# Cross-attention and RWKV layers on one core: GpSimd instead of VectorE computes the third bf16 piece of queries and keys

## The chip, the cores and the metric

The kernel runs on one core of a Trainium2 chip. The metric is the device time of one execution in microseconds (us); less is better. TensorE (PE) multiplies matrices and transposes, VectorE (DVE), ScalarE (ACT) and GpSimd (POOL) do the elementwise work, and SyncE (SP) issues nearly all DMAs. Each engine runs its own list of instructions strictly in order, and semaphores tie the lists together. A blocked instruction blocks everything behind it on its engine.

## The reference, cut to what matters

For each of 8 batches, layer 0 normalises x and the context (layer norm over 128 channels), makes queries, keys and values, does 16-head attention with softmax over 256 positions, and then a feed-forward block. Layer 1 is an RWKV layer: a learned token shift, receptance, key, value, gate and decay, a linear scan in time with an 8x8 state per head, group norm, gate, and a feed-forward block.

```
q = layer_norm(x + pos);  kv = layer_norm(ctx + pos)
Q, K, V = q @ Wq, kv @ Wk, kv @ Wv
ctx = softmax(Q @ K.T / sqrt(8)) @ V
r = ctx @ Wo + q;  x1 = gelu(layer_norm(r) @ W1 + b1) @ W2 + b2 + r
...
state = k*v + w*state;  out_t = r_t @ (u*k*v + state)     # 32 heads of 8, one step a token
```

The scores Q @ K.T are computed from bf16 pieces: Q and K (f32) are each split into three bf16 numbers, high, middle and low, and six products of such pieces are stacked along the contraction.

## The kernel before

The work of a batch is cut into five stages: a (normalise, queries, keys, values and their split), g (the maximum score of each row, the guard that keeps the exponential in range), h (scores, exponential, weighted sums, feed-forward), r (token shift, projections, scan) and o (read-out, group norm, feed-forward, store). The batches are pipelined: while batch n is in stage a or g, batch n-1 is in h and r, batch n-2 in o.

The order of work is written out by hand. `BEGIN` holds the tick at which each batch's stage begins, and `AT` the offset of each operation in its stage. Every engine's program walks through all ticks and emits what is due. A tick is no time: it decides only which instruction comes before which one on the same engine.

The split in stage a goes over four instructions, on 128x512 elements, queries and keys side by side. ACT `high` (L620) copies the product out of the PSUM bank `a_even` to `parts[:, 0]`. DVE `left` (L826) is the rest, `a_even - high`. ACT `middle` (L634) rounds it to `parts[:, 1]`. The last one, which this case is about, is the tensor_tensor of L829: `parts[:, 2] = left - parts[:, 1]`, f32 minus bf16 to bf16. SP's `spill` (L337) then copies the three pieces into `q_stack` and `k_stack` by 12 DMAs a batch, piece 2 last; it waits for the semaphore `s_parts` there.

On POOL stand, before the change: `zsum` (L774), the input plus positions, which is the first operation of stage a and which PE's `centre` (L397) waits for; `rstd_a`, `rstd_h`, `rstd_r`, `rstd_o` and `hrs` (powers of -0.5 on few elements); `kv` (L790, L791), and `rst_low` (L795).

PE's part that matters here is in this order in the first three batches: centre of batch 0, the rest of its stage a, centre and rest of stage a of batch 1, the 16 score pairs of stage g of batch 0 (L424, with DVE's row maxima `top`, L834, between them), the guard of batch 0, centre of batch 2. Before centre of batch 1 PE waits for three things:

```
pe.wait_ge(s_zsum, a.n + 1)
if a.n == 1:
    pe.wait_ge(s_left, 1)
    pe.wait_ge(s_v_padded, 1)
```

In stage r, DVE's `sx` (L882, the difference of neighbouring tokens, two inputs in SBUF), `xx` (L885) and PE's `maa1` (L509) follow one another; in stage o DVE's `yo` (L988) makes the output from two inputs in SBUF.

Of the kernel before, what the change touches and what calls it, by code (L numbers as in the profile page):

```python
# [9 lines left out]
ALU = mybir.AluOpType  # L10
# [36 lines left out]
for _n, _w in WEIGHTS:  # L47
# [17 lines left out]
        "SP": {"load": 0, "spill": (2322, 2430, 2430)},  # L65
        "PE": {"centre": 1792, "turn_nrm": 1951, "qk": 2014, "v": 2032},
        "ACT": {"dev": 1861, "nrm": 1920, "affine": 1985, "high": 2040, "v_pad": 2062, "middle": 2162},
        "POOL": {"zsum": 1726, "rstd_a": 1996},
        "DVE": {"var_a": 1808, "left": 2072, "parts": 2352},
    },  # L70
    "g": {
        "SP": {"guard": 380},
# [56 lines left out]
def due(at, engine, op, i=None):  # L129

    return PLACES.get((engine, op, i, at))


def ticks():

    times = [place[3] for place in PLACES]
    return range(min(times), max(times) + 1)


def build(nc, x, ctx_in, weights, vecs, pos, first, out):  # L140
    with ExitStack() as stack:
        def sb(name, shape, dt=F32):
            return stack.enter_context(nc.sbuf_tensor(name, shape, dt))
# [32 lines left out]
        def s0(batch):  # L176

            return initial[:, batch.n, 4:4 + 2 * S1].rearrange("p (h d) -> p h d", h=2)
# [3 lines left out]
        zsum = sb("zsum", [128, 2, T])  # L182
        devsq = sb("devsq", [128, 4, 128])
        squares = sb("squares", [128, 4])
        var_a = sb("var_a", [128, 4])
        rstd_a = sb("rstd_a", [128, 4])
# [3 lines left out]
        parts = sb("parts", [128, 3, 2, T], BF16)  # L190
        left = sb("left", [128, 2, T])
# [113 lines left out]
        def dma(batch, count=1):  # L305

            return batch.k * (16 * count) + 16 * count
# [446 lines left out]
        @block.gpsimd  # L754
        def _(pool):
            pool.memset(mhalf[:, :], -0.5).then_inc(s_setup, 1)
            pool.memset(th[:, :, :], 0.0).then_inc(s_setup, 1)
            for n in range(3):
                pool.memset(k_stack[n][:, :, :], 1.0).then_inc(s_setup, 1)
            for p in range(2):  # L760

                pool.memset(dec_rep[p][:, :, :, 0], 0.0).then_inc(s_zero, 1)

                pool.memset(yo[p][:, 0:1], 0.0).then_inc(s_stored[p], 16)
            pool.memset(x2[:, 0:1], 0.0).then_inc(s_done, 1)
            pool.wait_ge(s_const, CONSTS)
            pool.wait_ge(s_setup, SETUP)

            for at in ticks():
                if a := due(at, "POOL", "zsum"):  # L770
                    pool.wait_ge(s_x_in[a.p], dma(a, 2))
                    if a.n >= 1:
                        pool.wait_ge(s_centred, a.n)
                    pool.tensor_tensor(zsum[:, :, :], xin[a.p][:, :, :], pe_tab[:, None, :].broadcast_to([128, 2, T]), ALU.add).then_inc(s_zsum, 1)  # L774
                if a := due(at, "POOL", "rstd_a"):
                    pool.wait_ge(s_vareps, a.n + 1)
                    pool.tensor_tensor(rstd_a[:, :], var_a[:, :], mhalf[:, 0:4], ALU.pow).then_inc(s_rstd, 1)  # L777
                if h := due(at, "POOL", "rstd_h"):
                    pool.wait_ge(s_hvareps, h.n + 1)
                    pool.tensor_tensor(rstd_h[:, :], var_h[:, :], mhalf[:, 0:2], ALU.pow).then_inc(s_hrstd, 1)  # L780
                if r := due(at, "POOL", "rstd1"):
                    pool.wait_ge(s_var1, r.n + 1)
                    pool.tensor_tensor(rstd_r[:, :], var_r[:, :], mhalf[:, 0:1], ALU.pow).then_inc(s_rstd1, 1)
                for half in range(2):
                    if r := due(at, "POOL", "kv", half):
                        pool.wait_ge((s_v_rep_low, s_v_rep_high)[half], (r.n + 1) * 16)
                        pool.wait_ge(s_rk_sb, r.n + 1)
                        if r.n == 0:
                            pool.wait_ge(s_initial, 16)
                        pool.tensor_copy(kv[:, half, :, 0], s0(r)[:, half, :]).then_inc(s_kv, 1)  # L790
                        pool.tensor_tensor(kv[:, half, :, 1:NT], v_rep[:, half, :, 1:NT], rk[r.p][:, 1, half, None, 0:NT - 1].broadcast_to([128, S1, NT - 1]),  # L791
                                           ALU.mult).then_inc(s_kv, 1)
                if r := due(at, "POOL", "rst_low"):
                    pool.wait_ge(s_st, r.n * 2 + 1)
                    pool.tensor_tensor(st[:, 0, :, :], st[:, 0, :, :], rk[r.p][:, 0, 0, None, :].broadcast_to([128, S1, NT]), ALU.mult).then_inc(s_rst_low, 1)  # L795
                if o := due(at, "POOL", "hrs"):
                    pool.wait_ge(s_hvareps1, o.n + 1)
                    pool.tensor_tensor(hrs[:, :], hvar[:, :], mhalf[:, :], ALU.pow).then_inc(s_hrs, 1)  # L798
                if o := due(at, "POOL", "rstd2"):
                    pool.wait_ge(s_var2, o.n + 1)  # L800
                    pool.tensor_tensor(rstd_o[:, :], var_o[:, :], mhalf[:, 0:1], ALU.pow).then_inc(s_rstd2, 1)  # L801
# [3 lines left out]
        def _(dve):  # L805
# [14 lines left out]
            for at in ticks():  # L820
# [3 lines left out]
                if a := due(at, "DVE", "left"):  # L824
                    dve.wait_ge(s_high, a.n + 1)
                    dve.tensor_tensor(flat(left[:, :, :]), a_even[:, :], parts[:, 0].rearrange("p s t -> p (s t)"), ALU.subtract).then_inc(s_left, 1)  # L826
                if a := due(at, "DVE", "parts"):
                    dve.wait_ge(s_middle, a.n + 1)
                    dve.tensor_tensor(parts[:, 2], left[:, :, :], parts[:, 1], ALU.subtract).then_inc(s_parts, 1)  # L829

                for head in range(H0):
                    if g := due(at, "DVE", "top", head):
# [250 lines left out]
```

## Time and profile before

| what | value |
|---|---|
| device time, median of 3 runs | 441.82 us (441.0 to 442.71) |
| device time of the profiled execution | 440.58 us |
| its span in the profile | 438.4 us |
| TensorE | busy 72% of the span |
| VectorE | busy 65% of the span |
| ScalarE | busy 52% of the span |
| GpSimd | busy 36% of the span |
| mean granted clock of TensorE | 0.886 |

The span runs from the first to the last profiled instruction; the device time of the same execution is 2.2 us longer. In rows of the timeline a number xN behind an instruction means N of them merged, and the brackets at the end tell how long the engine had been idle and what ended the idle time.

### The profile page before, as it was taken

The page shows a single profiled execution, that of the slowest core. Times are in us where ns is not written, and L with a number is a line of the kernel's source. Part 1 is how long each engine was busy: PE and PEld are TensorE (multiplying, and loading weights), DVE is VectorE, ACT ScalarE, POOL GpSimd, SP SyncE. Part 2 cuts the span into 40 slices and gives each one's busy share as a digit, 9 for nine tenths or more (in the row PEclk, how much of TensorE's full clock was granted, in tenths as well). Part 3 has the DMA queues.
Part 4 walks back from the last instruction along what each step waited for, and adds up shares of the span by engine and source line. Part 5 has one row for each costly group of instructions (what it writes and reads, how often), then busy time and mean ns, then how long its engine had stood idle before and what let it go on. Part 6 is the DMA issues. An engine that isn't in the chain of part 4 may idle for free.

```text
span 438.4 us, 6463 instructions
## 1 busy us (share of the span) xinstructions
PE 317.3 (72%) x2320; PEld 203.3 (46%) x2320; DVE 285.3 (65%) x610; ACT 229.3 (52%) x585; POOL 158.4 (36%) x102
## 2 busy tenths in 40 slices
PE   1447587688598979896988798879878866664135
PEld 1321333455354655565555555555655554552013
DVE  5119057177569868985798698869877546747331
ACT  0540364763795488548845975665477564033010
POOL 6220200100754083428144614544072454417310
PEclk9965569699989999998999999989999998688555
DMA  8433020002600430061007000700400140041000
GB/s 243 203 98 88 27 55 20 1 25 62 122 24 1 113 70 1 1 143 40 2 1 168 27 0 21 176 0 2 110 13 2 22 99 0 0 106 40 0 0 12
DMA packets 23695, 23.44 MB, mean 53 GB/s; under 512 B 3568, under 2 KB 21360, under 8 KB 23536
## 3 DMA queue, kind: packets, MB, share of 16 engines
q1 hardware_dynamic: 23520, 19.57, 18.8%
q10 hardware_dynamic: 144, 3.47, 2.0%
q8 instruction: 18, 0.29, 0.3%
q14 instruction: 13, 0.11, 0.1%
HBM read 14.51 MB, written 2.10 MB: 38 GB/s over the span
## 4 chain that ended last, share of the span: by engine, by line
PE 43%; DVE 20%; ACT 17%; issue 15%; POOL 5%; POOLq 0%; ACTq 0%; DVEq 0%
PE o_bank L378 4%; PE h_sum L457 4%; DVE mixed L896 4%; DVE top L834 4%; PE r_one L371 4%; PE r_two L371 3%; PE h_even L490 3%; ACT L669 2%; ACT dec_rep L722 2%; PE r_one L384 2%; PE r_two L509 2%; DVE mixed L905 2%; ACT probs L643 2%; PE a_odd L424 2%; PE h_odd L445 2%
## 5 line engine op out<-in xcount | busy, mean ns | idle before, releaser
L798 POOL TENSOR_TENSOR hrs<-hvar,mhalf 128x32 f32<-128x32 f32 x8 | 43.5, 5439 | 52.3 <-DVE hvar L950 52.3
L834 DVE TENSOR_REDUCE top<-a_even 128x2 f32<-128x512 f32 x64 | 44.0, 687 | 11.4 <-PE a_even L424 6.3
L643 ACT ACTIVATE probs<-h_odd 128x512 f32<-128x512 f32 x64 | 38.3, 598 | 23.0 <-PE h_even L445 17.9
L834 DVE TENSOR_REDUCE top<-a_odd 128x2 f32<-128x512 f32 x64 | 43.9, 685 | 6.1 <-PE a_odd L424 5.8
L643 ACT ACTIVATE probs<-h_even 128x512 f32<-128x512 f32 x64 | 38.1, 595 | 14.3 <-PE h_odd L445 7.4
L927 DVE TENSOR_TENSOR_SCAN st<-dec_rep,v_rep 128x1024 f32<-128x1024 f32 x16 | 38.0, 2409 | 3.0 <-POOL v_rep L791 3.0
L791 POOL TENSOR_TENSOR v_rep<-v_rep,rk 128x1016 f32<-128x1016 f32 x16 | 37.6, 2348 | 0.0
L457 PE MATMUL h_sum<-probs,v_pad 128*32 128x256 f32 x512 | 35.1, 393 | 0.0
L795 POOL TENSOR_TENSOR st<-st,rk 128x1024 f32<-128x1024 f32 x8 | 30.2, 3770 | 7.6 <-DVE st L927 7.6
L424 PE MATMUL a_even<-k_stack,q_stack 62*128 62x256 bf16 x128 | 26.4, 289 | 6.0 <-DVE top L834 3.3
L424 PE MATMUL a_odd<-k_stack,q_stack 62*128 62x256 bf16 x128 | 26.5, 290 | 5.4 <-DVE top L834 5.4
L777 POOL TENSOR_TENSOR rstd_a<-var_a,mhalf 128x4 f32<-128x4 f32 x8 | 13.3, 1659 | 40.0 <-DVE var_a L823 40.0
L445 PE MATMUL h_odd<-q_stack,k_stack 64*128 64x256 bf16 x128 | 25.7, 282 | 1.3 <-ACT probs L643 0.9
L445 PE MATMUL h_even<-q_stack,k_stack 64*128 64x256 bf16 x128 | 25.7, 282 | 0.6 <-ACT probs L643 0.3
L801 POOL TENSOR_TENSOR rstd_o<-var_o,mhalf 128x1 f32<-128x1 f32 x8 | 4.4, 550 | 53.8 <-DVE var_o L967 53.8
L790 POOL COPY v_rep<-initial 128x8 f32<-128x8 f32 x16 | 4.6, 290 | 52.3 <-DMA v_rep<-values 27.6
L384 PE MATMUL r_one<-th,W 128*128 128x128 f32 x96 | 15.8, 304 | 6.8 <-ACT th L689 6.0
L826 DVE TENSOR_TENSOR left<-a_even,parts 128x512 f32<-128x512 f32 x8 | 5.5, 689 | 22.5 <-ACT parts L620 22.3
L397 PE MATMUL a_even<-W,zsum 128*128 128x128 f32 x64 | 10.9, 322 | 12.7 <-POOL zsum L774 8.0
L457 PEld LDWEIGHTS h_sum<-probs,v_pad 128*32 128x32 f32 x512 | 13.5, 110 | 13.0 <-issue 7.2
L384 PEld LDWEIGHTS r_one<-th,W 128*128 128x128 f32 x96 | 12.8, 203 | 10.8 <-ACT th L689 8.4
L780 POOL TENSOR_TENSOR rstd_h<-var_h,mhalf 128x2 f32<-128x2 f32 x8 | 5.8, 731 | 31.7 <-DVE var_h L857 31.6
(157 smaller groups left out, 778.0 us busy)
## 6 DMA issues: line engine op xcount, KB each, us to landing
v_rep<-values SPq DMA_DIRECT2D x16, 511.5 KB, 5.4
W<-in_weights ACTq DMA_DIRECT2D x1, 3392.0 KB, 11.5
q_stack<-parts SPq DMA_DIRECT2D x48, 64.0 KB, 3.4
k_stack<-parts SPq DMA_DIRECT2D x48, 64.0 KB, 2.7
xin<-in_x SPq DMA_DIRECT2D x8, 128.0 KB, 2.3
xin<-in_ctx SPq DMA_DIRECT2D x8, 128.0 KB, 2.7
values<-vt SPq DMA_DIRECT2D x8, 128.0 KB, 1.8
out<-yo SPq DMA_DIRECT2D x8, 128.0 KB, 3.9
```

Source lines behind the costliest of these rows:

```text
L371: mm = pe.matmul(dst[:, m * 128:(m + 1) * 128], w(name, half * E + m * 128, 128), src[:, half, :], start=half == 0, stop=half == 1)
L378: mm = pe.matmul(dst, src[:, half, :], w(name, half * E, E), start=half == 0, stop=half == 1)
L384: mm = pe.matmul(dst[:, half * 128:(half + 1) * 128], w(f"maa_w2_{group}", half * 128, 128), th[:, group // 4, :], start=True, stop=True)
L424: mm = pe.matmul(a_score[head % 2][:, j * T:(j + 1) * T], q_stack[g.ring][e:e + TOP_ROWS, head // 2, j * 128:(j + 1) * 128], k_stack[g.rin ...
L445: mm = pe.matmul(h_score[head % 2][:, j * T:(j + 1) * T], k_stack[h.ring][e:e + GUARD_ROWS, head // 2, j * 128:(j + 1) * 128], q_stack[h.r ...
L457: mm = pe.matmul(h_sum[quad * QUAD:(quad + 1) * QUAD, half * T:(half + 1) * T], v_pad[h.ring][:, j, HEAD_ORDER[four * 4 + quad], :], probs ...
L643: act.activation(flat(probs[turn % PROBS][:, :, :]), h_score[HEAD_ORDER[turn] % 2][:, :], ACT.Exp, scale=SCORE_SCALE).then_inc(s_probs, 1)
L791: pool.tensor_tensor(kv[:, half, :, 1:NT], v_rep[:, half, :, 1:NT], rk[r.p][:, 1, half, None, 0:NT - 1].broadcast_to([128, S1, NT - 1]), A ...
L795: pool.tensor_tensor(st[:, 0, :, :], st[:, 0, :, :], rk[r.p][:, 0, 0, None, :].broadcast_to([128, S1, NT]), ALU.mult).then_inc(s_rst_low, 1)
L798: pool.tensor_tensor(hrs[:, :], hvar[:, :], mhalf[:, :], ALU.pow).then_inc(s_hrs, 1)
L834: dve.tensor_reduce(top[:, :, H0 // 2 * (head % 2) + head // 2], a_score[head % 2][:, :].rearrange("p (a t) -> p a t", a=2), AX.X, ALU.max ...
L927: dve.tensor_tensor_scan(flat(st[:, half, :, :]), flat(dec_rep[r.p][:, half, :, :]), flat(kv[:, half, :, :]), 0.0, ALU.mult, ALU.add).then ...
```

## The change

The subtraction that makes the low piece leaves DVE's list and goes to POOL's, with the same operands, the same wait for `s_middle` and the same update of `s_parts`. Its offset in stage a changes from 2352 to 2478.

```
-        "POOL": {"zsum": 1726, "rstd_a": 1996},
-        "DVE": {"var_a": 1808, "left": 2072, "parts": 2352},
+        "POOL": {"zsum": 1726, "rstd_a": 1996, "parts": 2478},
+        "DVE": {"var_a": 1808, "left": 2072},
...
+                if a := due(at, "POOL", "parts"):
+                    pool.wait_ge(s_middle, a.n + 1)
+                    pool.tensor_tensor(parts[:, 2], left[:, :, :], parts[:, 1], ALU.subtract).then_inc(s_parts, 1)
...
-                if a := due(at, "DVE", "parts"):
-                    dve.wait_ge(s_middle, a.n + 1)
-                    dve.tensor_tensor(parts[:, 2], left[:, :, :], parts[:, 1], ALU.subtract).then_inc(s_parts, 1)
```

What this does to the lists: PE, ACT and SP keep theirs row for row, DVE's loses 8 rows and POOL's gains 8. POOL's list near the start, from the first zsum on, before the change (zsum of batch 0, rstd_a of batch 0, zsum of batch 1, and so on):

```order
15 L774 TENSOR_TENSOR zsum<-xin,pe_tab 128x512
16 L777 TENSOR_TENSOR rstd_a<-var_a,mhalf 128x4
17 L774 TENSOR_TENSOR zsum<-xin,pe_tab 128x512
18 L777 TENSOR_TENSOR rstd_a<-var_a,mhalf 128x4
19 L774 TENSOR_TENSOR zsum<-xin,pe_tab 128x512
```

The same place in the list of the changed kernel, where L780 is the moved subtraction:

```order
15 L774 TENSOR_TENSOR zsum<-xin,pe_tab 128x512
16 L777 TENSOR_TENSOR rstd_a<-var_a,mhalf 128x4
17 L780 TENSOR_TENSOR parts<-left,parts 128x512
18 L774 TENSOR_TENSOR zsum<-xin,pe_tab 128x512
19 L777 TENSOR_TENSOR rstd_a<-var_a,mhalf 128x4
20 L780 TENSOR_TENSOR parts<-left,parts 128x512
21 L774 TENSOR_TENSOR zsum<-xin,pe_tab 128x512
```

So parts of batch 0 now stands ahead of zsum of batch 1, and parts of batch 1 ahead of zsum of batch 2. From batch 2 on it stands behind the next batch's zsum, here for batch 4 (ahead of hrs of batch 0):

```order
37 L786 TENSOR_TENSOR rstd_r<-var_r,mhalf 128x1
38 L774 TENSOR_TENSOR zsum<-xin,pe_tab 128x512
39 L780 TENSOR_TENSOR parts<-left,parts 128x512
40 L801 TENSOR_TENSOR hrs<-hvar,mhalf 128x32
41 L804 TENSOR_TENSOR rstd_o<-var_o,mhalf 128x1
```

On DVE, the place from which parts of batch 3 is taken, before the change (the `top` rows are the row maxima of stage g of batch 2, `mixed` and `gate` are of stage r of batch 0):

```order
73 L834 TENSOR_REDUCE top<-a_odd 128x2
74 L905 TENSOR_TENSOR mixed<-mixed,xt 128x5x128 x2
75 L829 TENSOR_TENSOR parts<-left,parts 128x512
76 L834 TENSOR_REDUCE top<-a_even 128x2
77 L834 TENSOR_REDUCE top<-a_odd 128x2
78 L834 TENSOR_REDUCE top<-a_even 128x2
```

Without it, the maxima follow `mixed` directly; nothing else moves on DVE.

## Rows read from the trace of the kernel before

**Rows 1.** The page: busy time and share by engine; the last chain by engine.

```profile
PE 317.3 (72%) x2320; PEld 203.3 (46%) x2320; DVE 285.3 (65%) x610; ACT 229.3 (52%) x585; POOL 158.4 (36%) x102
...
PE 43%; DVE 20%; ACT 17%; issue 15%; POOL 5%; POOLq 0%; ACTq 0%; DVEq 0%
```

**Rows 2.** Timeline, 5 to 60 us: start us, length us, engine, line, operation.

```profile
6.57 1.26 POOL L774 TENSOR_TENSOR zsum<-xin,pe_tab 128x512 f32<-128x512 f32 x1
7.97 2.04 PE L397 MATMUL a_even<-W,zsum 128*128 128x128 f32 x8 [7.97 <-POOL zsum L774]
...
13.91 1.26 POOL L774 TENSOR_TENSOR zsum<-xin,pe_tab 128x512 f32<-128x512 f32 x1
...
20.86 0.63 ACT L634 ACTIVATE parts<-left 128x512 bf16<-128x512 f32 x1
...
21.08 1.13 PE L397 MATMUL a_even<-W,zsum 128*128 128x128 f32 x8 [0.75 <-ACT v_pad L628]
21.52 0.69 DVE L829 TENSOR_TENSOR parts<-left,parts 128x512 bf16<-128x512 f32 x1 [0.70 <-ACT parts L634]
...
45.13 2.05 PE L397 MATMUL a_even<-W,zsum 128*128 128x128 f32 x8 [1.04 <-DVE guard L842]
```

**Rows 3.** Same timeline, DVE in the maxima of batch 0.

```profile
36.77 0.69 DVE L834 TENSOR_REDUCE top<-a_odd 128x2 f32<-128x512 f32 x1
37.38 0.68 DVE L829 TENSOR_TENSOR parts<-left,parts 128x512 bf16<-128x512 f32 x1
...
37.98 0.69 DVE L834 TENSOR_REDUCE top<-a_even 128x2 f32<-128x512 f32 x1
```

**Rows 4.** Busy us (and instructions) by window; PEclk is TensorE's granted clock.

```profile
core 0: us, PE busy (x) PEld busy (x) DVE busy (x) ACT busy (x) POOL busy (x), PEclk, DMA share, GB/s
21.00:24.20 3.20, 1.13 (x8) 0.97 (x8) 0.86 (x2) 1.64 (x9) 0.53 (x1) 1.00 0.34 87
24.40:31.00 6.60, 3.98 (x12) 2.99 (x12) 0.12 (x1) 2.76 (x7) 1.52 (x2) 0.50 0.41 110
```

**Rows 5.** Timeline of DVE around parts of batch 3 and of batch 7.

```profile
101.36 0.69 DVE L829 TENSOR_TENSOR parts<-left,parts 128x512 bf16<-128x512 f32 x1
...
104.18 0.69 DVE L834 TENSOR_REDUCE top<-a_even 128x2 f32<-128x512 f32 x1 [0.94 <-PE a_even L424]
...
268.94 0.68 DVE L829 TENSOR_TENSOR parts<-left,parts 128x512 bf16<-128x512 f32 x1
...
270.47 0.69 DVE L834 TENSOR_REDUCE top<-a_even 128x2 f32<-128x512 f32 x1 [0.51 <-PE a_odd L424]
```

**Rows 6.** Timeline of ACT (middle of batch 6) and of POOL (hrs behind it).

```profile
216.79 0.65 ACT L634 ACTIVATE parts<-left 128x512 bf16<-128x512 f32 x1
...
219.97 5.44 POOL L798 TENSOR_TENSOR hrs<-hvar,mhalf 128x32 f32<-128x32 f32 x1 [6.32 <-DVE hvar L950]
```

**Rows 7.** Timeline of POOL and DVE: yo beside POOL's st, and alone.

```profile
162.90 3.55 POOL L795 TENSOR_TENSOR st<-st,rk 128x1024 f32<-128x1024 f32 x1
...
165.02 1.72 DVE L988 SCALAR_TENSOR_TENSOR yo<-y,x 128x256 f32<-128x256 f32 x1
...
207.92 0.55 DVE L988 SCALAR_TENSOR_TENSOR yo<-y,x 128x256 f32<-128x256 f32 x1
```

**Rows 8.** Timeline, middle, sx and maa1: batches 3 and 0, then 4 and 1.

```profile
89.98 0.63 ACT L634 ACTIVATE parts<-left 128x512 bf16<-128x512 f32 x1
...
91.40 0.42 DVE L882 TENSOR_TENSOR sx<-xt 128x256 f32<-128x256 f32 x1 [0.40 <-ACT xt L683]
...
91.86 0.61 DVE L885 SCALAR_TENSOR_TENSOR xx<-sx,vec,xt 128x128 f32<-128x128 f32 x2
...
92.53 0.60 PE L509 MATMUL r_two<-xx,W 128*128 128x128 f32 x3
...
129.55 0.62 ACT L634 ACTIVATE parts<-left 128x512 bf16<-128x512 f32 x1
...
131.04 0.42 DVE L882 TENSOR_TENSOR sx<-xt 128x256 f32<-128x256 f32 x1
...
132.24 0.38 PE L509 MATMUL r_two<-xx,W 128*128 128x128 f32 x1
```

**Rows 9.** The page, a costly group of POOL: busy us, mean ns.

```profile
L791 POOL TENSOR_TENSOR v_rep<-v_rep,rk 128x1016 f32<-128x1016 f32 x16 | 37.6, 2348 | 0.0
```

## The prediction

> **What bounds the kernel now.** I read the page first. No engine is full: TensorE is busy 72%, VectorE 65%, GpSimd 36% [rows 1]. So a change matters only where a wait ends last, and that has to be read place by place. The chain that ended last runs 43% over PE and 20% over DVE, and only 5% over POOL [rows 1]: on average POOL has room for one more instruction a batch, and DVE is the scarcer engine. An average says nothing of the place, however, so I went to the timeline next, at each of the eight places where parts leaves DVE and each of the eight where POOL takes it up. The places are of two kinds. In the first batches nothing is pipelined yet and everything hangs on one thread; from batch 2 on, four engines work on three batches at once.
>
> **The start, batch 0.** Before the change, zsum of batch 1 ran at 13.91 us, far ahead of its use; PE's centre of batch 1 started at 21.08, released by v_pad of batch 0 [rows 2]. In the changed order POOL has parts of batch 0 between rstd_a of batch 0 and that zsum. Parts waits for ACT's middle, which starts at 20.86 and takes 0.63, so it ends at 21.49 [rows 2]. POOL can start some 0.08 later (an estimate: a semaphore's hop), at 21.57. Queued behind the waiting instruction is zsum of batch 1, and behind that centre of batch 1, and PE's list has nothing else to offer.
>
> How long is parts on POOL? The trace has no such instruction there. The nearest row is zsum, two inputs, 512 elements: 1.26 us [rows 2]. Below it is half of kv, 2.348/2 = 1.17 us for 508 elements [rows 9]; above it half of st, 3.55/2 = 1.78 us [rows 7], which is lengthened by a neighbour. I take 1.26; the bf16 operand is not in any row, and 1.17 and 1.78 stay for the range. The Trainium skill (GPSIMD Engine Reference, section 3.1) gives 1.96 times DVE's duration for an f32 tensor_tensor; with this kernel's 0.69 us on DVE that would be 1.35, an estimate that would add 0.09 to the sum.
>
> So parts ends at 21.57 + 1.26 = 22.83, zsum of batch 1 at 22.83 + 1.26 = 24.09, and PE starts 0.14 later (zsum of batch 0 ended at 6.57 + 1.26 = 7.83, PE started at 7.97 [rows 2]), at 24.23 instead of 21.08: **+3.1 us**. Everything that follows on PE in these batches hangs on this: stage a of batch 1, then the maxima of batch 0, then guard, then centre of batch 2. I found nothing outside this thread that the work waits for here, so what is lost shifts the whole rest.
>
> **The clock at that place.** Centre of batch 1 took 1.13 us, while the same eight matmuls took 2.04 and 2.05 in batches 0 and 2 [rows 2]. The windows say why: granted clock 1.00, which is 2.4 GHz, from 21.0 to 24.2, after PE had been busy with stage a of batch 0, and 0.50, or 1.2 GHz, from 24.4 on, after PE had done only 1.13 us of work in those 3.2 us [rows 4]. The late centre starts at 24.2, after a stretch with no work at all. I expect it at the lower clock: 2.05 - 1.13 = **+0.9 us**. Its bounds are 0 and 0.9, as another execution may have its changes of clock elsewhere. That the cold stretch later on moves along with the work is an assumption that costs nothing either way on average.
>
> **Batch 1.** Here the move pays. In the maxima of batch 0 DVE goes from one top to the next without a gap: 36.77, parts at 37.38, top at 37.98 [rows 3]. Taking parts out brings the next top forward by 37.98 - 37.38 = **-0.6 us**, and the guard, which ends the stage, with it. On POOL, parts of batch 1 and zsum of batch 2 come later by some 13 us, but centre of batch 2 starts only at 45.13 and waits for DVE's guard [rows 2]: cover of 7 us and more, so nothing.
>
> **Batches 3 to 7, DVE.** Is the 0.6 earned again in each? After parts of batch 3 (101.36) DVE does two maxima and then stands idle for 0.94 us until PE delivers (104.18) [rows 5]. So without parts it would only stand idle for 1.5. The five batches look alike: within three rows behind parts DVE waits for PE or ACT, in batch 7 for 0.51 us (parts at 268.94, the waiting top at 270.47) [rows 5]. PE has the long block of projections in front of its next score pair, and that is what DVE waits for. Batch 2 is like that too. The gain there is nothing, with an upper bound of 0.6 each.
>
> **Batches 3 to 7, POOL.** Parts now waits for middle ahead of hrs. The tightest is batch 6: middle ends at 216.79 + 0.65 = 217.44, parts at 217.44 + 0.08 + 1.26 = 218.78, hrs starts at 219.97 [rows 6]. The cover is 1.2 us, and it would take an instruction of 2.4 us to use it up. SP issues piece 2 as early as before or earlier. Nothing.
>
> **A collision on the way.** yo, two inputs in SBUF, took 1.72 us when it started while POOL's st was running, and 0.55 when it was alone; it ended at 166.74, or 0.29 behind st's end at 166.45 [rows 7]. So a DVE instruction of this kind stands still until POOL's has finished. The moved instruction reads and writes SBUF all along, so whom does it meet? In batch 3 middle ends at 90.61, POOL has 90.69 to 91.95, and sx with its two inputs in SBUF starts at 91.40 [rows 8]. It would end at 91.95 + 0.28 = 92.23 instead of 91.82. xx ends at 92.47 and maa1 starts at 92.53 [rows 8], so 0.06 of the 0.41 is slack: +0.35. In batch 4 middle ends at 130.17, POOL has 130.25 to 131.51, sx starts at 131.04 and would end at 131.79 instead of 131.46: 0.33, less about 0.13 of slack ahead of maa1 at 132.24 [rows 8], +0.2. In batches 5 to 7 middle ends after sx has run, and I count nothing. Together **+0.55 us**, with bounds of 0 (sx is not held) and, with 1.78 us on POOL, some 0.5 more in each of the two, 1.6.
>
> The Trainium skill (SBUF — State Buffer, section "Who interferes with whom") says the same as a rule: a VectorE instruction with two SBUF inputs and a GpSimd instruction that reads SBUF share a port, and whoever starts first holds it for the whole instruction. It speaks against this change, and by it the term would be as above; without it the term would be 0 and the sum 3.4.
>
> **The sum.** 3.1 + 0.9 - 0.6 + 0.55 = 3.95, say +4.0 us. The profiled execution took 440.58 us (span 438.4): it would take 444.6 (span 442.4). It lies 1.2 below the median of the runs shown, 441.82; the median becomes **445.8 us**, or 0.9% more. What a measurement of this kernel can tell from no change is about 0.5%, or 2.2 us.
>
> **The rivals.**
> 1. Only the wait at the start counts: the clock's change falls kindly and sx is not held. Then 3.1 - 0.6 = +2.5, so 444.3, and some slack that I took for none may take a part: 443.0 to 444.3, around the border of 0.5%. For it: the clock is seen in one execution, the collision is read from another instruction. Chance 0.17.
> 2. The other side: DVE is the bound after all. If the 0.6 is earned in each of the seven batches 1 to 7 (every row that follows parts moves PE's next block), the move is worth 7 x 0.6 = 4.2, against 3.1 at the start: -1.1, so 440.7, faster though hard to measure. It decides if DVE's gaps behind parts are gaps that PE owes to an earlier maximum. Against it are the gaps of 0.94 and 0.51 us, which end with PE's matmuls that stand behind a block without a gap [rows 5]. Chance 0.05.
> 3. The subtraction is slow on POOL with bf16 operands, 1.78 us or more, and meets more DVE instructions. Then the start costs 3.6, the collisions 1.6: 3.6 + 0.9 - 0.6 + 1.6 = +5.5, so 447.3 and up. For it: no row has bf16 on POOL. Chance 0.08.
>
> My forecast holds the remaining 0.70, from 444.3 to 447.
>
> **How the numbers follow.** The predicted time is that of the forecast, 445.8. The range goes down to 443.3, into rival 1, and up to 447.6, into rival 3; rival 2 and the tails stay out. Slower by over 0.5% (above 444.0): the forecast, rival 3, and a little of rival 1, 0.79. Within 0.5%: most of rival 1, half of rival 2 and what I overlook, 0.17. Faster: 0.04.
>
> **What would show it.** In the changed kernel's profile POOL's parts of batch 0 starts at about 21.6 and lasts 1.2 to 1.8, zsum of batch 1 ends near 24.1, and PE's second centre starts near 24.2, released by POOL, and takes 2.05 (right) or 1.13 (no clock term). Centre of batch 2 starts near 48.5 instead of 45.13; if it starts at 46 or before, the start is wrong. sx of batch 0 and of batch 1 takes about 0.8 instead of 0.42. Behind the place of parts DVE's gaps are longer by 0.6. The distance from centre of batch 2 to the end stays within 1 us of the old one; should it shrink by 3 us, rival 2 is right.

## The result, and the profile after

The changed kernel took 446.56 us (median of 4 runs, 446.06 to 448.43), the kernel before 441.41 in the runs beside it: ratio 1.0102, with a 95% interval of 1.0058 to 1.0146. Run once more with other runs of before beside it, it gave 1.0145 (1.0111 to 1.0179), 447.89 against 442.04 us. It is slower, by 5 to 6 us (5.15 and 5.85).

The page of the changed kernel, busy time by engine, is hardly different from that of before [rows 1]: DVE has 8 instructions and 5 us less, POOL 8 instructions and 9 us more. The averages don't show where the 5.6 us more of span are from.

```profile
span 444.0 us, 6463 instructions
PE 320.5 (72%) x2320; PEld 205.8 (46%) x2320; DVE 280.2 (63%) x602; ACT 229.1 (52%) x585; POOL 167.4 (38%) x110
L780 POOL TENSOR_TENSOR parts<-left,parts 128x512 bf16<-128x512 f32 x8 | 9.2, 1156 | 39.9 <-ACT parts L634 39.9
```

The third line is the moved instruction among the costly groups: 1.16 us on POOL, and POOL sat idle for 39.9 us in all ahead of it, waiting for ACT's middle. Idle time of POOL costs nothing by itself. It costs where something needed is queued behind. The timeline of the start, which answers to [rows 2], shows that place:

```profile
20.87 0.63 ACT L634 ACTIVATE parts<-left 128x512 bf16<-128x512 f32 x1
21.58 1.15 POOL L780 TENSOR_TENSOR parts<-left,parts 128x512 bf16<-128x512 f32 x1 [7.63 <-ACT parts L634]
22.69 1.26 POOL L774 TENSOR_TENSOR zsum<-xin,pe_tab 128x512 f32<-128x512 f32 x1
24.00 2.07 PE L397 MATMUL a_even<-W,zsum 128*128 128x128 f32 x8 [3.67 <-POOL zsum L774]
...
48.99 2.05 PE L397 MATMUL a_even<-W,zsum 128*128 128x128 f32 x8 [1.04 <-DVE guard L842]
```

POOL stands still from 13.95 to 21.58, since parts of batch 0 waits at the head of its queue. zsum of batch 1, which ran at 13.91 before, runs at 22.69, and the releaser of PE's second centre is now POOL's zsum instead of ACT's v_pad: 24.00 instead of 21.08. The third centre starts at 48.99 instead of 45.13. Between these two executions the start is thus 3.9 us longer; how much of that is the change and how much the clock that each of them happened to have is worked out below.

Two more places answer to rows of before. DVE around the place of parts of batch 3 and batch 7, as in [rows 5]:

```profile
107.13 0.69 DVE L834 TENSOR_REDUCE top<-a_even 128x2 f32<-128x512 f32 x1 [1.55 <-PE a_even L424]
...
276.05 0.69 DVE L834 TENSOR_REDUCE top<-a_even 128x2 f32<-128x512 f32 x1 [0.84 <-PE a_odd L424]
```

The gaps were 0.94 and 0.51 and are now 1.55 and 0.84. DVE is done earlier and waits the longer for PE (in batch 7, DVE's next instruction, agg, also waits 0.17 for ACT). And parts, sx and maa1 in batches 3/0 and 4/1, as in [rows 8]:

```profile
93.33 1.16 POOL L780 TENSOR_TENSOR parts<-left,parts 128x512 bf16<-128x512 f32 x1 [1.89 <-ACT parts L634]
94.04 0.73 DVE L882 TENSOR_TENSOR sx<-xt 128x256 f32<-128x256 f32 x1 [0.40 <-ACT xt L683]
...
95.48 1.27 PE L509 MATMUL r_two<-xx,W 128*128 128x128 f32 x8 [0.32 <-DVE xx L885]
...
134.41 1.16 POOL L780 TENSOR_TENSOR parts<-left,parts 128x512 bf16<-128x512 f32 x1 [1.55 <-ACT parts L634]
...
135.21 0.64 DVE L882 TENSOR_TENSOR sx<-xt 128x256 f32<-128x256 f32 x1
```

sx takes 0.73 and 0.64 instead of 0.42. Both times it ends 0.28 us behind POOL's parts (94.77 behind 94.49, 135.85 behind 135.57).

### The profile page after: what moved, and what is told of

It is laid out like the page before. It is cut to its first block, busy times and chain, and to the rows that moved or that the text cites. A ratio compares the mean times of both kernels' runs of the same rounds, so it can differ in the third digit from the quotient of the medians.

```text
span 444.0 us, 6463 instructions
## 1 busy us (share of the span) xinstructions
PE 320.5 (72%) x2320; PEld 205.8 (46%) x2320; DVE 280.2 (63%) x602; ACT 229.1 (52%) x585; POOL 167.4 (38%) x110
## 4 chain that ended last, share of the span: by engine, by line
PE 43%; DVE 19%; ACT 18%; issue 14%; POOL 5%; POOLq 0%; ACTq 0%; DVEq 0%
PE o_bank L378 4%; DVE mixed L896 4%; PE h_sum L457 4%; DVE top L834 4%; PE r_one L371 4%; PE r_two L371 3%; PE h_even L490 3%; ACT L669 2%; ACT dec_rep L722 2%; PE r_one L384 2%; PE r_two L509 2%; DVE mixed L905 2%; ACT probs L643 2%; PE h_odd L445 2%; ACT devsq L603 2%
## 5 line engine op out<-in xcount | busy, mean ns | idle before, releaser
L780 POOL TENSOR_TENSOR parts<-left,parts 128x512 bf16<-128x512 f32 x8 | 9.2, 1156 | 39.9 <-ACT parts L634 39.9
L777 POOL TENSOR_TENSOR rstd_a<-var_a,mhalf 128x4 f32<-128x4 f32 x8 | 13.3, 1659 | 26.3 <-DVE var_a L826 26.3
L397 PE MATMUL a_even<-W,zsum 128*128 128x128 f32 x64 | 11.8, 342 | 15.6 <-POOL zsum L774 11.6
L829 DVE TENSOR_TENSOR left<-a_even,parts 128x512 f32<-128x512 f32 x8 | 5.5, 690 | 22.6 <-ACT parts L620 22.2
L603 ACT ACTIVATE devsq<-a_even 128x128 f32<-128x128 f32 x32 | 8.3, 277 | 19.6 <-PE a_even L397 19.6
```

## The experiments

Theory: the loss is made at one place, zsum of batch 1 waiting behind parts of batch 0. Rivals: POOL's slower instruction and its meetings with DVE cost all along the pipeline; or DVE's relief gives something back there.

**e8_pool_0_first** is the kernel before with parts of batch 0 alone moved, to the same place as in the change. **e2_wait_only** moves nothing and only makes POOL wait at that place.

```
# e8_pool_0_first, against the changed kernel
-                if a := due(at, "POOL", "parts"):
+                if (a := due(at, "POOL", "parts")) and a.n in (0,):
...
+                if (a := due(at, "DVE", "parts")) and a.n not in (0,):
# e2_wait_only, against the kernel before, ahead of zsum
+                    if a.n in (1, 2):
+                        pool.wait_ge(s_parts if a.n == 1 else s_middle, a.n)
```

> The kernel before with parts of batch 0 alone on POOL, ahead of zsum of batch 1 as in the change; all other parts on DVE at their old places. If the start makes the whole loss: second centre at 24.0, +2.9 us and +0.9 of clock, so +3.9 us, 445 to 446, ratio 1.008 to 1.011, about what the whole change costs. Rival: less than half of it, under 443.5.

> The kernel before, parts on DVE, with two waits more on POOL: zsum of batch 1 waits for parts of batch 0 on DVE, zsum of batch 2 for middle of batch 1. Nothing is moved. Start theory: parts of batch 0 ends on DVE at 22.2, zsum of batch 1 at 23.6, the second centre starts at 23.7 instead of 21.1, at the lower clock: +2.6 and +0.9, so +3.5 us, 444.5 to 445.5, ratio 1.007 to 1.010. Rival (the loss comes from the instruction on POOL): no change, 441 to 442.

e8 gave a ratio of 1.0096 (1.0058 to 1.0134), 446.18 us: one instruction of eight, moved, costs as much as the first measurement of the whole change (1.0102), though less than the second (1.0145). e2 gave 1.0070 (1.0042 to 1.0097), 444.51 us, with no work moved at all. Its timeline (in this kernel's line numbers parts on DVE is L831, zsum L776):

```profile
21.53 0.69 DVE L831 TENSOR_TENSOR parts<-left,parts 128x512 bf16<-128x512 f32 x1 [0.70 <-ACT parts L634]
22.39 1.26 POOL L776 TENSOR_TENSOR zsum<-xin,pe_tab 128x512 f32<-128x512 f32 x1 [8.45 <-DVE parts L831]
23.70 2.08 PE L397 MATMUL a_even<-W,zsum 128*128 128x128 f32 x8 [3.38 <-POOL zsum L776]
```

It is 0.3 us less late than the change, as DVE's parts is 0.47 shorter than POOL's and the hop to POOL a little longer. So of the 2.92 us by which the changed kernel's second centre is late, 2.62 come with the wait in POOL's queue alone, and 0.30 with the instruction being on POOL.

**e1_order** undoes nothing but the order: on POOL, parts of batches 0 and 1 goes behind the next zsum.

```
                     for batch in BATCHES:
-                        yield (engine, op, i, BEGIN[stage][batch.n] + offset), batch
+                        late = 200 if (op == "parts" and batch.n < 2) else 0
+                        yield (engine, op, i, BEGIN[stage][batch.n] + offset + late), batch
```

> The changed kernel with one thing undone: on POOL, parts of batches 0 and 1 stands behind zsum of the next batch instead of ahead of it (batches 2 to 7 as in the change). Start theory: the loss comes from zsum of batch 1 waiting behind parts of batch 0. Then the second centre is back near 21.1 us at the high clock, centre of batch 2 near 44.7 (0.2 to 0.6 earlier than before, since DVE's maxima have no parts between them), and the time is 0 to 1 us over before, by the collisions alone: 441 to 442.5, ratio 0.998 to 1.003. Rival (POOL's slower instruction and its collisions with DVE make the loss all along): it stays near the changed kernel, 444 to 446.5, ratio over 1.006.

1.0021 (0.9986 to 1.0055), 442.95 us: no difference that can be told, with all eight parts on POOL. In its profile (centre is L398 here) centre is back, released by v_pad:

```profile
13.93 1.26 POOL L775 TENSOR_TENSOR zsum<-xin,pe_tab 128x512 f32<-128x512 f32 x1
...
21.10 1.13 PE L398 MATMUL a_even<-W,zsum 128*128 128x128 f32 x8 [0.75 <-ACT v_pad L629]
```

One part of the expectation failed: its third centre starts at 45.15 and not near 44.7, no earlier than in the first trace of before (45.13). The section on the clock says why.

**e3_pool_2to7** and **e5_left_out** look at the pipelined part: parts on POOL in batches 2 to 7 alone (as e8, with that set and DVE for the rest); and parts of batches 2 to 7 on no engine.

```
# e5_left_out, against the kernel before
-                if a := due(at, "DVE", "parts"):
+                if (a := due(at, "DVE", "parts")) and a.n < 2:
...
-                        sp.wait_ge((s_high, s_middle, s_parts)[part], a.n + 1)
+                        sp.wait_ge((s_high, s_middle, s_parts if a.n < 2 else s_middle)[part], a.n + 1)
```

> Parts of batches 0 and 1 stays on DVE, that of batches 2 to 7 is on POOL as in the change. Start theory: the start is as before, the collisions with sx in batches 3 and 4 cost 0.3 and 0.2 us, DVE's relief is worth nothing: +0.5 us, 441.4 to 442.9, ratio 0.999 to 1.004. Rival of relief (every parts taken from DVE is worth 0.6): -3 us, 438 to 439, ratio 0.993. Rival of collisions: over 444.

> The kernel before without parts of batches 2 to 7 at all, on no engine (the third piece of those batches is that of batch 1, so the output is not the reference's); SP waits for middle in its place. It measures DVE's relief alone, without POOL and without collisions. Theory that DVE waits for PE behind each of these places: no change, -0.3 to +0.3 us, 441 to 442, and the gaps of DVE behind the place are longer by 0.6. Rival: 0.6 each, -3.0 to -3.6 us, 438, ratio 0.992.

0.9991 (0.9963 to 1.0020) and 0.9994 (0.9964 to 1.0024). Six instructions of 0.68 us taken off the engine that is busy 65% of the span are worth nothing that can be measured, whether POOL has them or nobody; the intervals leave room for 0.4%, not for the 0.8% that 0.6 us each would make. e5's DVE shows why; the gap of batch 3, where it was 0.94 [rows 5]:

```profile
100.47 0.69 DVE L834 TENSOR_REDUCE top<-a_even 128x2 f32<-128x512 f32 x1
101.08 0.69 DVE L834 TENSOR_REDUCE top<-a_odd 128x2 f32<-128x512 f32 x1
103.30 0.69 DVE L834 TENSOR_REDUCE top<-a_even 128x2 f32<-128x512 f32 x1 [1.54 <-PE a_even L424]
```

**e7_pool_1** moves parts of batch 1 alone (POOL, behind zsum of batch 2), the one place where relief should pay.

```
# e7_pool_1, against the changed kernel, with e1's shift by 200
-                if a := due(at, "POOL", "parts"):
+                if (a := due(at, "POOL", "parts")) and a.n in (1,):
...
+                if (a := due(at, "DVE", "parts")) and a.n not in (1,):
```

> The kernel before with parts of batch 1 alone on POOL, behind zsum of batch 2. It is the one place where my theory gives DVE's relief a worth: the maxima of batch 0 lose one instruction of 0.6 us. Expected: centre of batch 2 starts 0.6 earlier (44.5 instead of 45.1) and the time falls by 0.2 to 0.6 us, 441.0, inside the noise. Rival (PE's two score matmuls at the low clock limit the maxima too): 0 to 0.2 us.

1.0004 (0.9978 to 1.0030): as expected not to be told from no change. The trace does tell it, and it says 0.4, not 0.6. In this kernel and in a second trace of the kernel before (**e11_before_again**, no edit) TensorE is at its lower clock through all the maxima of batch 0 (how this is read is said under the table):

> The kernel before once more, for a second trace and as a measure of what the timing cannot tell. Second centre at 21.1; it was at the high clock in the first trace, and at the low one in three of the five experiments that leave it at 21.1. If the clock's term of +0.9 is luck of the execution, centre can take 2.05 here too. Ratio 1.000.

e11 gave 1.0004 (0.9977 to 1.0030), which is what the timing can tell. Its DVE in the maxima:

```profile
36.70 0.68 DVE L834 TENSOR_REDUCE top<-a_odd 128x2 f32<-128x512 f32 x1
37.48 0.69 DVE L834 TENSOR_REDUCE top<-a_even 128x2 f32<-128x512 f32 x1
38.09 0.68 DVE L834 TENSOR_REDUCE top<-a_odd 128x2 f32<-128x512 f32 x1
38.69 0.68 DVE L829 TENSOR_TENSOR parts<-left,parts 128x512 bf16<-128x512 f32 x1
39.29 0.69 DVE L834 TENSOR_REDUCE top<-a_even 128x2 f32<-128x512 f32 x1
```

Without parts the step from an odd top to the next even one is 0.78 (36.70 to 37.48), because it waits for PE's score pair; with parts between them it is 1.20 (38.09 to 39.29). The difference, 0.42, is what parts costs. From the first top's start to the last one's end it is 11.45 us with it (33.30 to 44.75) and 11.03 without in e7.

**The clock of the second centre.** The table has what the profiled executions show: the start of the second centre, whether it ran at 2.4 GHz (ACT's next instruction starts 1.16 to 1.20 us behind centre's start) or at 1.2 GHz (2.01 to 2.12 behind); centre is four calls in f32, recorded as eight matmuls; further, the start of the third centre, the length of sx of batches 0 and 1, the granted clock of TensorE from 155 to 185 us, and the time from hvar of batch 0 to hvar of batch 1.

| kernel | 2nd centre | its clock | 3rd centre | sx | clock 155:185 | hvar 0 to 1 | span |
|---|---|---|---|---|---|---|---|
| before | 21.08 | high | 45.13 | 0.42, 0.42 | 1.00 | 41.81 | 438.40 |
| e11_before_again | 21.07 | low | 46.45 | 0.43, 0.42 | 1.00 | 41.79 | 440.30 |
| e1_order | 21.10 | high | 45.15 | 0.73, 0.65 | 1.00 | 41.73 | 441.47 |
| e3_pool_2to7 | 21.08 | low | 46.46 | 0.73, 0.65 | 1.00 | 41.74 | 438.75 |
| e5_left_out | 21.08 | high | 45.54 | 0.42, 0.42 | 1.00 | 41.81 | 438.89 |
| e7_pool_1 | 21.09 | low | 46.06 | 0.42, 0.42 | 1.00 | 41.81 | 440.88 |
| e4_no_meeting | 21.08 | low | 46.06 | 0.43, 0.41 | 1.00 | 41.80 | 440.36 |
| e9_best | 21.09 | low | 46.06 | 0.43, 0.42 | 1.00 | 41.82 | 440.63 |
| e2_wait_only | 23.70 | low | 48.70 | 0.42, 0.41 | 1.00 | 41.82 | 442.09 |
| e8_pool_0_first | 24.03 | low | 49.33 | 0.43, 0.42 | 1.00 | 41.82 | 441.73 |
| e13_late_34 | 24.02 | low | 49.02 | 0.43, 0.42 | 1.00 | 41.81 | 441.04 |
| changed kernel | 24.00 | low | 48.99 | 0.73, 0.64 | 0.94 | 43.04 | 443.97 |
| e10_after_again | 24.01 | low | 49.01 | 0.73, 0.64 | 0.94 | 42.47 | 446.61 |
| e6_pe_busy | 24.01 | high | 47.68 | 0.74, 0.65 | 0.89 | 42.22 | 445.44 |

Where centre starts at 21.1, three executions of eight had it at the high clock; where it starts at 23.7 or 24.0 behind an idle PE, none of five.

Why are the levels read from ACT's start and not from the granted clock? Because ahead of a trace's first fall the column prints 1.00 in any case. Two windows of e11, with the first and the second centre (the granted clock is the third figure from the end):

```profile
8.00:10.20 2.20, 2.02 (x8) 1.72 (x8) 0.30 (x5) 0.07 (x1) 0.00 (x0) 1.00 0.79 333
21.00:24.20 3.20, 2.05 (x8) 1.78 (x8) 0.69 (x1) 1.53 (x9) 0.00 (x0) 1.00 0.34 87
```

Both say 1.00, and both centres took the 2.0 us of the lower clock. In e11 and in the changed kernel the column shows no fall before 64 us; their long low stretch at the start is missing from it, and so their mean granted clock comes out too high (0.918 in both, against 0.886 in the first trace of before).

A fall in the column, on the other hand, says that the clock was high before it. Five of the 14 traces have one between 23.8 and 27.3 us: before, e1, e5, e8 and e6. The other nine, both traces of the changed kernel among them, have none before 38 us. Here are e8 and then e6, the kernel with more for PE to do (below):

```profile
20.80:24.20 3.40, 0.17 (x1) 0.17 (x2) 0.06 (x1) 0.72 (x3) 2.37 (x2) 1.00 0.32 80
24.20:27.20 3.00, 1.80 (x8) 1.51 (x8) 0.00 (x0) 1.14 (x8) 0.00 (x0) 0.50 0.41 106
...
20.80:24.20 3.40, 1.59 (x14) 1.40 (x13) 0.05 (x1) 0.71 (x3) 2.37 (x2) 1.00 0.32 81
24.20:27.20 3.00, 0.97 (x8) 0.78 (x7) 0.17 (x1) 1.14 (x8) 0.57 (x1) 1.00 0.41 105
```

In e8 PE did 0.17 us of work from 20.80 to 24.20, the clock fell, and the late centre took 1.98. That is the prediction's mechanism, in one trace. In the changed kernel's own two traces there is no such fall: by its length centre ran low there, as it did in five of the eight traces in which it is not late. The traces of the five put the rise before that fall at 20.4 to 20.9 us, and up to 20.1 us PE has the same work in all 14, so which of the two cases an execution is in is not the change's doing.

**e6_pe_busy** gives PE eight more calls to do in the wait (16 in the record).

```
                 if a := due(at, "PE", "centre"):
+                    if a.n == 1:
+                        for _ in range(8):
+                            pe.matmul(r_two[:, 0:128], w("Wq"), w("Wk"), start=True, stop=True)
                     pe.wait_ge(s_zsum, a.n + 1)
```

> The changed kernel with 8 more matmuls (128x128x128, f32) on PE ahead of the second centre, into a PSUM bank that is not in use yet; their result is not used. PE has them while it would wait for zsum of batch 1. Clock theory: the second centre took 2.05 us instead of 1.13 because PE had done nothing since 20.3; with PE busy the clock is still high at 24.0 and centre takes 1.13, so -0.9 us against the changed kernel at centre of batch 2 (48.1 instead of 49.0), or more if the maxima run at the high clock too. If the clock falls all the same: centre at 2.05, no gain, or a loss of up to 0.5 where the last of the 8 end after 24.0.

Its timeline (the extra matmuls are L392, centre L400, parts L783, zsum L777):

```profile
20.13 2.06 PE L392 MATMUL r_two<-W 128*128 128x128 f32 x16
21.59 1.15 POOL L783 TENSOR_TENSOR parts<-left,parts 128x512 bf16<-128x512 f32 x1 [7.63 <-ACT parts L637]
22.70 1.26 POOL L777 TENSOR_TENSOR zsum<-xin,pe_tab 128x512 f32<-128x512 f32 x1
24.01 1.16 PE L400 MATMUL a_even<-W,zsum 128*128 128x128 f32 x8 [1.81 <-POOL zsum L777]
```

With PE busy until 22.2, centre at 24.01 runs at the high clock (1.16 us), and the third centre starts at 47.68, or 1.3 us earlier than in the changed kernel. Against e8, the other late trace that was at the high clock at 21 us, the clock goes as the theory has it, in one trace of each. The time does not follow: 1.0109 (1.0060 to 1.0159), 447.19 us. The gain of 1.3 us at 48 us is gone again at the end of the span, 445.44.

The third centres of the table fit together once the clock is set apart. At the same clock, parts of batch 1 taken off DVE brings it forward by 0.39: 45.15 in e1 against 45.54 in e5, and 46.06 against 46.45. The 45.13 of the first trace of before is 0.41 earlier than e5, which does the same work up to there: in before the granted clock was 1.00 again from 31.2 to 34.4 us, in e5 0.50 from 29 to 45. That is why e1's third centre was not earlier than that of before.

**The meetings with sx.** **e4_no_meeting** is e1 with a wait more, **e13_late_34** the changed kernel with the same wait:

```
                 if a := due(at, "POOL", "parts"):
                     pool.wait_ge(s_middle, a.n + 1)
+                    if a.n in (3, 4):
+                        pool.wait_ge(s_xx1, a.n - 2)
```

> As e1_order, and parts of batches 3 and 4 on POOL also waits until xx of batches 0 and 1 has run on DVE, so that it meets neither sx nor xx. Collision theory: sx takes 0.42 in all batches (0.73 and 0.64 in the changed kernel for batches 0 and 1), and the distance from sx of batch 0 to hvar of batch 0 shortens by 0.5 us against e1_order; the time is 0.5 below it, which the timing may not resolve. Rival (the lengthened sx is no cost, slack takes it up): maa1 starts as in e1_order.

> The changed kernel, start and all, but parts of batches 3 and 4 on POOL waits until xx of batches 0 and 1 has run, so that it meets neither sx nor xx. The changed kernel measured 1.010 and 1.0145, parts of batch 0 alone 1.0096. If the collisions make the difference between these, the ratio is 1.007 to 1.010 here. By the rows they cost 0.5 us: 1.009 to 1.013, not to be told from the changed kernel. If it is 1.012 or more, the collisions are not what the changed kernel has on top of the start. Centre of batch 2 at 49.0 in any case, sx of batch 0 takes 0.42.

In both sx takes 0.41 to 0.43 again, e13's in batch 0:

```profile
93.78 0.43 DVE L884 TENSOR_TENSOR sx<-xt 128x256 f32<-128x256 f32 x1 [0.39 <-ACT xt L683]
```

e4 gave 1.0024 (0.9995 to 1.0054), the same as e1 with the meetings (1.0021): with the early start they cost nothing that can be told. The distance that e4's expectation names, from sx to hvar of batch 0, can be told, but only at the same clock. It is 45.15 us in e1 and 43.35 in e4, and most of that is not the meetings:

| granted clock, 115 to 130 us | sx not held | sx held |
|---|---|---|
| 0.89 | 43.34 to 43.36 (before, e11, e2, e4) | 43.82, 43.89 (e10, e6) |
| 0.77 | 44.93 to 44.97 (e5, e7, e8, e9) | 45.11 to 45.20 (changed kernel, e1, e3) |

So the meetings of sx lengthen this distance by 0.5 us in one row and by 0.2 in the other. (e13, 43.62 at 0.77 with sx not held, fits neither row.) e3's trace shows one way in which the clock decides: there TensorE ran its score pairs at 1.2 GHz ahead of maa1 (granted clock 0.50 from 89.7 to 92.9), and maa1 (L510 in this kernel) had to wait for them and not for xx, which had ended at 91.43:

```profile
91.53 0.63 PE L425 MATMUL a_even<-k_stack,q_stack 62*128 62x256 bf16 x2
92.09 1.15 PE L510 MATMUL r_two<-xx,W 128*128 128x128 f32 x4
```

e13 gave 1.0074 (1.0041 to 1.0106), 444.98 us, with the late start (third centre at 49.02) and no meetings of sx. That is less than the changed kernel's 1.0102 and 1.0145, and below the second of them beyond both intervals. **e10_after_again** is that second one, no edit; 1.010 was expected of it, and its centre took 2.08:

> The changed kernel once more, for a second trace of its start and more runs. Second centre at 24.0 in every execution; in the one trace so far at the lower clock. Where the clock's changes fall at other times in this execution, centre may take 1.1 instead of 2.05, and centre of batch 2 starts at 48.1 instead of 49.0. Ratio to before again 1.010.

With the late start, then, the meetings seem to cost more than 0.5 us: 1 to 3 us against e13, but 0.3 to 2.2 against e8, which has the late start and no meetings too (1.0096, from 6 executions), and whose interval overlaps both measurements of the change. The table's last columns show part of it: in the three traces that have both the late start and the meetings of sx, and in none of the eleven others, the granted clock falls once more between 155 and 185 us, and the stretch from hvar of batch 0 to hvar of batch 1 takes 42.2 to 43.0 instead of 41.7 to 41.8. The windows of the changed kernel, of e10 and of e13 (busy us by engine, the granted clock third from the end), each from 155 to 185 us:

```profile
155.00:185.00 30.00, 24.89 (x181) 17.16 (x181) 21.90 (x48) 21.00 (x58) 17.39 (x11) 0.94 0.22 45
```

```profile
155.00:185.00 30.00, 25.69 (x181) 18.01 (x180) 23.57 (x48) 21.93 (x60) 17.06 (x11) 0.94 0.25 53
```

```profile
155.00:185.00 30.00, 24.77 (x200) 15.94 (x202) 24.32 (x52) 22.64 (x61) 20.29 (x11) 1.00 0.15 33
```

**e9_best** is what the experiments point to: parts of batch 0 on DVE, the others on POOL, that of batch 1 behind zsum of batch 2 (as in e7), those of batches 3 and 4 behind xx (as in e4).

```
-                if a := due(at, "POOL", "parts"):
+                if (a := due(at, "POOL", "parts")) and a.n in (1, 2, 3, 4, 5, 6, 7):
                     pool.wait_ge(s_middle, a.n + 1)
+                    if a.n in (3, 4):
+                        pool.wait_ge(s_xx1, a.n - 2)
```

> What the experiments point to: parts of batch 0 on DVE, of batches 1 to 7 on POOL, that of batch 1 behind zsum of batch 2, those of batches 3 and 4 behind xx. The maxima of batch 0 are 0.4 us shorter, sx is nowhere held, the rest is as before: -0.4 us, 441.4, ratio 0.998 to 1.001, at the edge of what can be told. A rival with relief in all batches: ratio 0.993.

1.0023 (0.9997 to 1.0049), 442.74 us: it lies above the range expected of it and does not beat the kernel before. Its third centre is 0.4 earlier than that of e11 at the same clock (46.06 against 46.45), and the end does not show it.

## Why the prediction was right, step by step

The direction and the place were right, and the time, 446.56 against 445.8 predicted, lies in the range; the second measurement, 447.89, lies 0.3 above it.

- **The wait at the start, +3.1.** Shown by e8, e2 and e1. It measured 2.92 (24.00 against 21.08). The step was right; POOL's parts took 1.15 where 1.26 was taken from zsum, below the 1.17 that was its lower bound.
- **The clock, +0.9.** The mechanism is borne out by one trace each of e8 and e6, but the size was read from one execution. The second trace of before has the low clock as well (third centre at 46.45), and nothing shows that the changed kernel's two traces were at the high clock before the wait. With three of eight executions at the high clock when the start is early, and none of five when it is late behind an idle PE, the term is worth 0.9 x 3/8, or 0.3 to 0.4 on average (an estimate, from few executions). The prediction named 0 as its lower bound and took the upper one.
- **Batch 1, -0.6.** Mis-sized: 0.42. The prediction took DVE to run without a gap and overlooked that PE's score pair, at the low clock, is due there too; it had the step of 0.60 from a pair of rows, where the step without parts would be 0.78 every second time. The first trace of before has that step too, two rows on (38.58 to 39.36).
- **Batches 3 to 7, DVE, 0.** Right: e5 and e3, no difference, and the gaps are longer (1.55 and 0.84, so by 0.6 and 0.3, the latter with 0.17 ahead of agg). Rival 2, relief in every batch, is out.
- **Batches 3 to 7, POOL's cover, 0.** Right. Parts of batch 6 ends at 224.26 and hrs starts at 225.75 in the changed kernel. But the same instruction is in the way of DVE's att (L943), which is ahead of hvar and has both its inputs in SBUF:

```profile
223.11 1.15 POOL L780 TENSOR_TENSOR parts<-left,parts 128x512 bf16<-128x512 f32 x1 [3.87 <-ACT parts L634]
223.93 0.62 DVE L943 SCALAR_TENSOR_TENSOR att<-hsum,att 128x256 f32<-128x256 f32 x1
225.75 5.44 POOL L801 TENSOR_TENSOR hrs<-hvar,mhalf 128x32 f32<-128x32 f32 x1 [1.49 <-DVE hvar L950]
```

- **The collision, +0.55.** It happened at the two places named, and by the lengths of sx it is 0.31 + 0.22 = 0.53. There is a third, which the prediction missed: for batches 5 to 7 it looked at sx alone and counted nothing. In batch 6 att took 0.62 and ended 0.29 behind parts (224.55 behind 224.26). It took 0.61 or 0.62 in all eight kernels traced that have parts of batch 6 on POOL, e4 and e13 among them, and 0.42 in the six that don't; hvar of batch 2 is 0.2 later for it (43.31 to 43.33 us behind that of batch 1 in the changed kernel, e3, e4, e9 and e13; 43.12 to 43.14 in before, e2, e8 and e11). What the time makes of the collisions is another matter: nothing to be told from those of sx with the early start (e1 against e4), more than the 0.5 with the late one (the changed kernel against e13 and e8).
- **The signs.** The third centre was to start near 48.5 and started at 48.99: 2.92 for the wait, 0.94 for the second centre's clock, 0.41 for the high stretch that the first trace of before had in its maxima, less 0.4 for batch 1. The distance from there to the end was to stay within 1 us of the old one; it grew from 393.3 to 395.0, and to 397.6 in e10. The forecast had no term for that.

Worked out anew, between executions whose second centre runs at the same low clock: the span of the changed kernel is 443.97 - 440.30 = 3.7 us over e11's. The start has 48.99 - 46.45 = 2.5 of it, and hvar 0 to hvar 1 43.04 - 41.79 = 1.25. Measured over all runs the difference is 5 to 6 us, of which the rows account for 2.5 (start) + 0.35 (clock of the second centre) + 0.2 to 0.5 (sx) + 0.2 (att) + 0.4 to 1.25 (hvar 0 to hvar 1, with the further fall of the clock), or 3.7 to 4.8. That the forecast of +4.0 came so near has some luck in it: the clock's term at the second centre was too large, and the one later in the kernel and att's meeting were not foreseen.

**What stays open.** Why the late start and the meetings together bring one more low stretch of the clock is not shown; there are three traces with both, and all three have it. Nor is it shown that this stretch is what the time is lost by: from hvar of batch 1 to that of batch 2 it takes 41.6 us in e5 and e7 and 44.3 in e6, so that differences as large come and go at other places. What the rows leave of the 5 to 6 us, 0.4 to 2.2 us, is in no row that I can name. No kernel with a start that is later still was measured, so that the start has no slack is read from the rows alone. The distance from the third centre to the end varies from 392.0 (e13) to 397.8 us (e6), and in the two traces of before it is 393.3 and 393.9.

## What to carry to other kernels

Before an instruction is given to an engine with time to spare, look at what stands behind it in that engine's queue at the place where it waits, above all in the first iterations, where nothing else is in flight: a wait of 7.6 us at the head of POOL's queue made PE's next block 2.9 us late and the kernel 4 us slower (e8), and one place later it cost nothing that could be told. Relief of a busy engine is worth only what the next wait behind it leaves: six instructions of 0.68 us taken away altogether gave nothing that could be measured. Where the moved instruction lands, look at every instruction of the other engine beside it, not at the one that you thought of. And a term read from one execution, such as which clock a stretch had, should be weighed by how often other executions have it.

## What was not expected of the hardware

- POOL's subtraction with a bf16 operand and a bf16 result took 1.15 us for 128x512, less than the f32 sum of the same size (1.26 us); on DVE the same subtraction takes 0.68.
- A DVE instruction with two inputs in SBUF does not always stand still beside POOL. In the changed kernel `mixed` (L905, twice 128x640) took its usual 0.8 us each time beside POOL's hrs, a power on 128x32 elements, which is recorded until 272.75: the first of the two lies wholly inside it, the second, from 272.25, for 0.5 us. The Trainium skill (SBUF — State Buffer, section "Who interferes with whom") has the port held for the whole instruction; that agrees with sx and att beside parts and not with these rows, as far as POOL's recorded spans can be trusted.

```profile
267.31 5.44 POOL L801 TENSOR_TENSOR hrs<-hvar,mhalf 128x32 f32<-128x32 f32 x1 [1.89 <-DVE hvar L950]
...
271.52 1.55 DVE L905 TENSOR_TENSOR mixed<-mixed,xt 128x640 f32<-128x640 f32 x2
```
